# Normalisation work shared out anew, Mamba weights loaded earlier, and feed-forward chunks overlapped in an eight-block kernel

## What is computed

```python
x = x + _layernorm(_L0_attn_ref(_layernorm(x), ...))   # gated delta rule
x = x + _layernorm(_L0_ffn_ref(_layernorm(x), ...))    # window attention + gelu feed-forward, 2 layers
x = x + _layernorm(_L1_attn_ref(_layernorm(x), ...))   # attention on Pluecker lines
x = x + _layernorm(_L1_ffn_ref(_layernorm(x), ...))    # ternary feed-forward, 512 hidden
x = x + _layernorm(_L2_attn_ref(_layernorm(x), ...))   # attention
x = x + _layernorm(_L2_ffn_ref(_layernorm(x), ...))    # experts
x = x + _layernorm(_L3_attn_ref(_layernorm(x), ...))   # two Mamba passes, forwards and backwards
x = x + _layernorm(_L3_ffn_ref(_layernorm(x), ...))    # int8 feed-forward, 384 hidden
```

```python
# ternary
h = silu(_tlin(x, w1_w, w1_s)) * _tlin(x, w2_w, w2_s)
h = gelu(_tlin(h, h1_w, h1_s)); h = gelu(_tlin(h, h2_w, h2_s)); return _tlin(h, w3_w, w3_s)
# int8
h = silu(x @ wg.T) * (x @ wu.T); return h @ wd.T
# window feed-forward
a, g = split(h @ w1 + b1); x = x + (a * gelu(g)) @ w2 + b2
# Mamba, before its scan
xp, z = split(x @ W_in.T); xc = silu(conv(xp) + conv_b); dt_lo, Bm, Cm = split(xc @ W_xp.T)
dt = softplus(dt_lo @ W_dt.T + dt_b)
```

## Time and profile before

| | us |
|---|---|
| median of 3 runs | 4943.62 |
| lowest, highest | 4943.38, 4948.53 |
| profiled execution | 4947.78 |
| its span in the trace | 4945.9 |
| both Mamba scans, of the span | 1625 |
| seven normalisations, first to last instruction, 23.1 to 25.7 each | about 165 |
| four feed-forward stages touched | about 310 |
| two `mamba_inputs` | about 175 |

### The profile page before, as it was taken

How to read it: one execution, slowest core, us unless ns; L and a number is a source line. 1 busy time by engine, 2 the same in 40 slices (tenths; PEclk the granted TensorE clock), 3 DMA queues, 4 the chain that set the end, 5 groups by cost and what they waited for, 6 DMA issues and landing times. The chain is left out here.

```text
span 4945.9 us, 76468 instructions
## 1 busy us (share of the span) xinstructions
PE 3930.8 (79%) x20245; PEld 2366.6 (48%) x20365; DVE 3734.1 (75%) x6293; ACT 2549.7 (52%) x5336; POOL 2926.6 (59%) x2821
## 2 busy tenths in 40 slices
PE   5888888888578577576979964788888868888884
PEld 3666666666456356365447742333333323333332
DVE  5777777777377378366048857899999889999995
ACT  3555555555344244323246654566666456666662
POOL 2555555555454144143013344899999579999991
PEclk8999999989778878788999987999999989999997
DMA  1000000000000000000000000000000000000000
GB/s 50 9 9 8 9 9 9 8 9 8 16 0 0 21 0 0 12 0 24 0 18 1 1 14 10 0 0 0 0 0 0 8 0 0 0 0 0 0 0 14
DMA packets 90089, 33.37 MB, mean 7 GB/s; under 512 B 78032, under 2 KB 86113, under 8 KB 88929
## 3 DMA queue, kind: packets, MB, share of 16 engines
q1 hardware_dynamic: 89824, 30.17, 2.5%
HBM read 24.89 MB, written 5.24 MB: 6 GB/s over the span
## 5 line engine op out<-in xcount | busy, mean ns | idle before, releaser
L3284 POOL TENSOR_TENSOR dBx<-dtx,b_row 128x1024 f32<-128x1024 f32 x512 | 1219.4, 2382 | 3.9 <-ACT b_row L3250 3.9
L3318 DVE TENSOR_TENSOR_SCAN h<-banks,dBx 128x1024 f32<-128x1024 f32 x512 | 1168.5, 2283 | 19.2 <-ACT banks L3244 19.2
L3202 PE MATMUL banks<-hc,ident 128*128 128x512 f32 x2048 | 964.4, 593 | 0.0
L3244 ACT ACTIVATE banks<-dt,A 128x510 f32<-128x510 f32 x1024 | 661.7, 682 | 4.2 <-DVE h L3318 3.5
L3250 ACT ACTIVATE b_row<-banks 128x512 f32<-128x512 f32 x512 | 305.9, 597 | 574.8 <-PE banks L3186 574.8
L3202 PEld LDWEIGHTS banks<-hc,ident 128*128 128x128 f32 x2048 | 388.5, 190 | 272.3 <-issue 246.8
L3326 DVE TENSOR_TENSOR hc<-h,banks 128x768 f32<-128x768 f32 x512 | 478.6, 935 | 10.8 <-ACT c_row L3255 6.6
L3186 PE MATMUL banks<-bc_lo,selectors 128*128 128x512 bf16 x1024 | 391.3, 382 | 73.8 <-POOL b_row L3273 64.7
L3293 POOL TENSOR_TENSOR hc<-h,c_row 128x256 f32<-128x256 f32 x512 | 376.7, 736 | 55.9 <-ACT c_row L3255 28.7
L3185 PE MATMUL banks<-bc_hm_c,selectors 128*128 128x512 bf16 x506 | 195.1, 385 | 186.0 <-DVE hc L3326 185.6
L3185 PEld LDWEIGHTS banks<-bc_hm_c,selectors 128*128 (+1 forms) x512 | 49.2, 96 | 434.8 <-issue 434.5
(11 more groups left out here) (447 smaller groups left out, 9238.7 us busy)
## 6 DMA issues: line engine op xcount, KB each, us to landing
delta_blocks<-A_turned SPq DMA_DIRECT2D x256, 8.0 KB, 1.5
inv_turned<-delta_blocks SPq DMA_DIRECT2D x256, 8.0 KB, 1.8
blocks<-delta_blocks SPq DMA_DIRECT2D x32, 64.0 KB, 2.1
delta_blocks<-blocks_inv SPq DMA_DIRECT2D x32, 64.0 KB, 1.9
wh<-in_l1f_wh SPq DMA_DIRECT2D x1, 2048.0 KB, 9.0
wqkv<-in_l0f_wqkv SPq DMA_DIRECT2D x2, 768.0 KB, 4.1
residual<-in_x SPq DMA_DIRECT2D x1, 1024.0 KB, 4.7
wv<-in_l0a_wv SPq DMA_DIRECT2D x1, 1024.0 KB, 7.3
```

Source lines behind the costliest of these rows:

```text
L3202: i = nc.tensor.matmul(k.bank[e], k.ident[:], hc[:, s, e, :], start=False, stop=False)
L3244: i = nc.scalar.activation(a3[:, :, 1:], d3[:, :, 1:], ACT.Exp, scale=mem["A"][:, e, bass.ds(n, 1)])
L3284: nc.gpsimd.tensor_tensor(dBx[:, s % NS], dtx[:, :, bass.ds(c * SCH, SCH)], across(bsb[:, s % NS, :], SE), ALU.mult).then_inc(q["dbx_ready ...
L3318: v.tensor_tensor_scan(flat(h[:, s % NS]), flat(k.banks[:, at:at + SE, :]), flat(dBx[:, s]), 0.0, ALU.mult, ALU.add).then_inc(q["scanned"], 1)
```

## The change

- **Normalisation.** POOL no longer adds groups 0 and 2 into `X`; the DVE does, with a drain behind. POOL does all four powers of round 0 ahead of its first add. ACT applies only groups 0 and 1 of round 1; the DVE applies groups 2 and 3, and signals a new semaphore `applied_late`, on which PE waits. ACT makes its four copies behind its last application.
- **`ffn_int8` and `window_ffn_layer`.** Loops are written out. PE multiplies gate and up of chunk c+1 ahead of the down projection of chunk c; the wait for `out` moves to the down projection, and each gate-and-up block waits for the product of the chunk before that reads its banks. `hid` has two copies. The DVE moves a chunk out behind the products of the next.
- **`ffn_ternary`.** On PE only: the loop is written out, the up block (bank 4 + ob) goes ahead of the gate block, so that only the second product of a chunk waits for the move out of bank 0; and each layer waits for the blocks of its input one by one, within its first output block.
- **Mamba.** The weights of both passes (13 transfers) are issued by SP during the second normalisation, into memories of their own. The DVE adds one, multiplies dt by x and by the skip factor chunk by chunk; POOL keeps only its part of the split. ACT's logs of chunks 0 and 1 go ahead of chunk 3's copies, the exps of chunk 3 ahead of the log of chunk 2.

```diff
             def _(pool):
...
                 powers(0, 0)
                 powers(0, 1)
                 powers(0, 2)
-                add(0)
                 powers(0, 3)
                 add(1)
                 powers(1, 0)
-                add(2)
                 powers(1, 1)
                 add(3)
...
+                def add(g):
+                    dve.wait_ge(applied, g + 1)
+                    nc.vector.tensor_tensor(k.X[:, cols(g), :], k.X[:, cols(g), :], k.H[:, cols(g), :], ALU.add)
+                    dve.drain()
+
+                def apply(g):
+                    dve.drain()
+                    for t in tiles(g):
+                        i = nc.vector.tensor_scalar(k.H[:, t, :], k.X[:, t, :], rstd[:, 1, t:t + 1], shift[:, 1, t:t + 1],
+                                                    ALU.mult, ALU.add)
+                    i.then_inc(applied_late, 1)
...
                 apply(1, 0)
-                for g in range(1, NG):
-                    apply(1, g)
-                    copy_turned(g - 1)
-                copy_turned(NG - 1)
+                apply(1, 1)
+                for g in range(NG):
+                    copy_turned(g)
...
-                with pe.Fori(0, NCH) as c:
-                    x = k.HT[:, bass.ds(c * bpc, bpc), PAD:PAD + T]
-                    pe.wait_ge(out, c + 1)
+                for c in range(NCH):
+                    x = k.HT[:, c * bpc:(c + 1) * bpc, PAD:PAD + T]
                     for ob in range(KB):
-                        for j in range(2):
+                        for j in (1, 0):
+                            if ob == 0 and j == 0:
+                                pe.wait_ge(out, c + 1)
...
-                        pe.wait_ge(*((prod, c * KB + KB) if l == 0 else (gelu[0], c * KB + KB)))
                         for ob in range(KB):
                             for kb in range(KB):
+                                if ob == 0:
+                                    pe.wait_ge((prod, gelu[0])[l], c * KB + kb + 1)
...
+                for c in range(NCH):
+                    gate_and_up(c)
+                    if c > 0:
+                        down_projection(c - 1)
+                down_projection(NCH - 1)
...
         with Part(k) as p:
-            mem = mamba_memories(p)
+            mem = mamba_memories(k, p)
+            normalise(k, src=k.H, affine=affine[:, 0], meanwhile=lambda sp: load_mamba_weights(k, sp, mem))
...
                 exps(1)
+                logs(0)
+                logs(1)
                 high(3)
                 exps(2)
-                logs(0)
-                logs(1)
+                exps(3)
                 logs(2)
-                exps(3)
                 logs(3)
...
-                split(0)
-                split(1)
-                one_plus(0)
-                split(2)
-                one_plus(1)
-                split(3)
-                one_plus(2)
-                scaled_x(0)
-                scaled_x(1)
-                one_plus(3)
-                scaled_x(2)
+                for c in range(SNC):
+                    split(c)
```

More of the change, by code:

```diff
@@ L198, in _ @@
                 shift_of(0, 2)
+                add(0)
+                statistics(1, 0)
                 shift_of(0, 3)
-                statistics(1, 0)
                 statistics(1, 1)
                 shift_of(1, 0)
+                add(2)
                 statistics(1, 2)
@@ L453, in _, with move_out @@
             def _(dve):
[L454 removed]
                 dve.wait_ge(loaded, 32)
                 nc.vector.tensor_scalar(w[:], wi[:], 1.0 / 127.0, None, ALU.mult).then_inc(scaled, 1)
[L457 removed]
+                def move_out(c):
+                    dve.wait_ge(down, c + 1)
+                    nc.vector.tensor_copy(k.Y[:, c * (CH // P):(c + 1) * (CH // P), :],
+                                          k.bank[6][:].rearrange("p (t d) -> p t d", d=D)).then_inc(out, 1)
+                for c in range(NCH):
                     for ob in range(KB):
                         dve.wait_ge(gated, c * KB + ob + 1)
[L460 removed]
+                        nc.vector.tensor_tensor(hid[:, c % 2, ob, :], k.bank[KB + ob][:], gate[:, ob, :],
                                                 ALU.mult).then_inc(prod, 1)
[L462 to L464 removed]
+                    if c > 0:
+                        move_out(c - 1)
+                move_out(NCH - 1)
 def lay_out_experts(i, d, np):
@@ L1760, in _, with down_projection @@
                         i.then_inc(pair, 1)
-                    pe.wait_ge(prod, c * KB + KB)
+                def down_projection(c):
+                    if c > 0:
+                        pe.wait_ge(out, c)
                     for tt in range(CH // P):
                         for kb in range(KB):
-                            i = nc.tensor.matmul(k.bank[6][:, tt * D:(tt + 1) * D], hid[:, kb, tt * P:(tt + 1) * P],
+                            if tt == 0:
+                                pe.wait_ge(prod, c * KB + kb + 1)
+                            i = nc.tensor.matmul(k.bank[6][:, tt * D:(tt + 1) * D], hid[:, c % 2, kb, tt * P:(tt + 1) * P],
                                                  w2[:, kb, :], start=kb == 0, stop=kb == KB - 1)
                     i.then_inc(down, 1)
+                for c in range(NCH):
+                    both_parts(c)
+                    if c > 0:
+                        down_projection(c - 1)
+                down_projection(NCH - 1)
             @block.scalar
@@ L1770, in _ @@
                 act.wait_ge(loaded, 64)
-                with act.Fori(0, NCH) as c:
+                for c in range(NCH):
                     for ob in range(KB):
                         act.wait_ge(pair, c * KB + ob + 1)
+                        if c > 0:
+                            act.wait_ge(prod, (c - 1) * KB + ob + 1)
                         nc.scalar.activation(gate[:, ob, :], k.bank[KB + ob], ACT.Gelu, bias=b1[:, 1, ob:ob + 1]).then_inc(gated, 1)
@@ L1781, in _, with add_out @@
                 dve.drain()
-                with dve.Fori(0, NCH) as c:
+                def add_out(c):
+                    dve.wait_ge(down, c + 1)
+                    y = k.Y[:, c * (CH // P):(c + 1) * (CH // P), :]
+                    nc.vector.tensor_tensor(y, k.bank[6].rearrange("p (t d) -> p t d", d=D), y, ALU.add).then_inc(out, 1)
+                for c in range(NCH):
                     for ob in range(KB):
                         dve.wait_ge(gated, c * KB + ob + 1)
-                        nc.vector.scalar_tensor_tensor(out=hid[:, ob, :], in0=k.bank[ob], scalar=b1[:, 0, ob:ob + 1],
+                        nc.vector.scalar_tensor_tensor(out=hid[:, c % 2, ob, :], in0=k.bank[ob], scalar=b1[:, 0, ob:ob + 1],
                                                        in1=gate[:, ob, :], op0=ALU.add, op1=ALU.mult).then_inc(prod, 1)
-                    dve.wait_ge(down, c + 1)
-                    y = k.Y[:, bass.ds(c * (CH // P), CH // P), :]
-                    nc.vector.tensor_tensor(y, k.bank[6].rearrange("p (t d) -> p t d", d=D), y, ALU.add).then_inc(out, 1)
+                    if c > 0:
+                        add_out(c - 1)
+                add_out(NCH - 1)
 def lay_out_delta(i, d, np):
@@ L2769, in lay_out_mamba, with load_mamba_weights @@
     d["l3a_sel"] = np.stack([np.concatenate([e, e]), np.concatenate([e, z]), np.concatenate([z, e])], 1)
+def load_mamba_weights(k, sp, m):
+    for n in (1, 2):
+        for dst, src in m[n]["loads"]:
+            sp.dma_start(dst[:], src).then_inc(m["loaded"], 16)
+    sp.dma_start(m["self"][:], k.dram["l3a_sel"]).then_inc(m["loaded"], 16)
 def bi_mamba(k, add_y):
@@ L2830, with mamba_memories @@
 CPAD = 3
-def mamba_memories(p):
+def mamba_memories(k, p):
     m = {}
```

122 lines of the change are left out of this document (57 added, 65 removed).

## The result

The changed kernel took 4856.44 us (median of 4 runs, 4850.64 to 4866.03) where the kernel before took 4943.50 (4 runs, 4933.74 to 4948.53). The ratio is 0.9831, interval 0.9812 to 0.9849: about 87 us less. The forecast was 4861 with a range of 4847 to 4881, so time and direction were right. The profiled execution took 4854.47, with a span of 4852.3 (before 4945.9).

What follows compares the result with a forecast made beforehand. Bound: PE's idle time between matmul groups in feed-forward, hand-overs among DVE, POOL and ACT in normalisations. Feed-forward 27.6, ternary 15.4, normalisation 28.7, Mamba loads 8.1, softplus 3.0: 82.8 us off 4943.62, so 4861, range 4847 to 4881.

Steps and rivals of the forecast that it cites:

- the worse end: Mamba softplus: gain between 4 and -0.5 us a pass; the forecast took 1.5, nearer the lower, 3.0 in all.

## What to carry to other kernels

Where an engine is busy for 78 to 90% of a stage, as PE was here, and idles only at hand-overs, issue the next chunk's independent work ahead of the dependent step: each wait that is covered was worth its whole idle time here, and the price was a second copy of the buffer. For an instruction that meets another engine's, multiply the number of meetings by what one of that size costs, taken from a row, rather than assume the worse end. Where the time scatters by more than an edit is worth, judge the edit by the length of its own stage, cut at the same instructions in both traces, and check an untouched stage beside it.

## What the hardware showed that was not expected

Stages that lean on PE change length from execution to execution of the same program, by 4 to 12 us in the gated delta stage and the first window attention, with the same work on the other engines; normalisations repeat to 0.1. In the window attention the granted clock goes with it (0.81 and 0.84). Smaller pieces do it too: the first eight matmuls of the first Mamba inputs took 5.21 us in the changed kernel and 3.67 in its repeat, at granted clocks of 0.69 and 1.00, which is the whole difference of 1.5 between their stages.

```profile
2944.46 5.21 PE L2950 MATMUL banks<-norm_featmajor,win 128*128 128x512 f32 x8 [1.28 <-DVE xp_padded L3148]
```

```profile
2936.25 3.67 PE L2950 MATMUL banks<-norm_featmajor,win 128*128 128x512 f32 x8 [1.28 <-DVE xp_padded L3148]
```

And a wait in a written-out loop is met a little sooner than the same wait in a loop with a register: 0.92 against 1.03 at a chunk's start, 1.90 against 2.21 at the stage's.
